# Moving the sign bytes and the taps forward, computing the second double's convolution with three products, and swapping P3 and P7 at the end

## The reference

```python
out = lax.conv_general_dilated(x, weight, window_strides=(1,), padding=[(4, 4)], feature_group_count=4)  # 9 taps
out = out + jnp.einsum('nd,od->no', cond, c_weight)[:, :, None] + bias[None, :, None]
w = kernel.astype(x.dtype) * 2.0 - 1.0            # kernel: (1024, 1024) booleans, so signs +1 and -1
return x + scale * jnp.einsum('bsi,if->bsf', out, w)
```

## Time and profile before

| | us |
|---|---|
| three runs | 174.07, 175.43, 176.49 |
| median | 175.43 |
| the profiled execution | 174.09 |
| its span (first to last instruction) | 172.2 |
| TensorE busy in it | 164.2 |
| VectorE, ScalarE, POOL busy | 136.9, 71.8, 37.6 |

### The profile page before, as it was taken

How to read it: one execution, slowest core, us unless ns; L and a number is a source line. 1 busy time by engine, 2 the same in 40 slices (tenths; PEclk the granted TensorE clock), 3 DMA queues, 4 the chain that set the end, 5 groups by cost and what they waited for, 6 DMA issues and landing times.

```text
span 172.2 us, 2765 instructions
## 1 busy us (share of the span) xinstructions
PE 164.2 (95%) x914; PEld 136.6 (79%) x914; DVE 136.9 (79%) x180; ACT 71.8 (42%) x68; POOL 37.6 (22%) x43
## 2 busy tenths in 40 slices
PE   7699999999999999999999999999999999999791
PEld 2378888998888779887998889887988899888580
DVE  4735493996999999779986899779977997699461
ACT  3201996470791148521781069304842340214000
POOL 4230600005040334006400343043400540000000
PEclk9969999999999999999999999999999999999999
DMA  5688697777799877887977888988888666414006
GB/s 205 139 159 248 249 196 196 125 200 188 143 337 237 256 153 306 184 229 189 297 185 176 262 173 306 225 249 112 331 214 204 94 249 138 105 49 199 0 0 244
DMA packets 27486, 33.38 MB, mean 194 GB/s; under 512 B 3537, under 2 KB 19857, under 8 KB 27473
## 3 DMA queue, kind: packets, MB, share of 16 engines
q1 hardware_dynamic: 22176, 25.63, 54.6%
q10 hardware_dynamic: 4912, 6.78, 14.8%
q0 software_dynamic: 384, 0.81, 2.2%
HBM read 10.06 MB, written 8.40 MB: 107 GB/s over the span
## 4 chain that ended last, share of the span: by engine, by line
PE 92%; DMA 3%; DVE 2%; issue 1%; ACTq 1%; DVEq 0%
PE ps_A L828 30%; PE ps_conv L809 18%; PE ps_C L828 15%; PE ps_conv L786 9%; PE ps_B L828 8%; DMA taps_nat<-weight 3%; PE ps_B L845 2%; PE ps_C L845 2%; PE ps_toep L845 2%; PE ps_A L845 2%; PE ps_toep L828 1%; PE ps_toep L765 1%; PE ps_C L776 1%; PE ps_A L753 1%; DVE sums L250 1%
## 5 line engine op out<-in xcount | busy, mean ns | idle before, releaser
L485 ACT CAST hi<-sums 128x1024 fp32r<-128x1024 f32 x14 | 14.7, 1049 | 44.5 <-DVE sums L622 38.4
L401 POOL TENSOR_TENSOR set<-x_blk 128x512 f32<-128x512 f32 x12 | 17.3, 1461 | 69.7 <-DMA x_blk<-x_phase 69.7
L643 DVE SCALAR_TENSOR_TENSOR x_nat<-ps_A,scale_col,x_nat 128x512 f32<-128x512 f32 x27 | 20.2, 748 | 15.0 <-PE ps_A L828 14.2
L442 ACT COPY x_phase<-x_nat 128x1032 f32<-128x1032 f32 x13 | 27.2, 2135 | 2.2 <-DMA x_nat<-x 2.2
L828 PE MATMUL ps_A<-sign_T,hi 128*128 128x512 f32 x80 | 22.4, 401 | 0.9 <-DVE x_nat L643 0.9
L485 ACT CAST hi<-y_sum 128x1024 fp32r<-128x1024 f32 (+1 forms) x14 | 11.7, 834 | 25.8 <-DMA y_sum<-y_two 16.5
L828 PE MATMUL ps_A<-sign_T,lo 128*128 128x512 f32 x80 | 22.0, 396 | 0.0
L828 PEld LDWEIGHTS ps_A<-sign_T,lo 128*128 128x128 f32 x80 | 15.0, 188 | 3.8 <-DVE lo L632 0.3
L828 PEld LDWEIGHTS ps_A<-sign_T,hi 128*128 128x128 f32 x80 | 14.5, 189 | 4.2 <-issue 1.3
L809 PE MATMUL ps_conv<-toeplitz,w_bytes 128*128 128x128 f32 x144 | 17.2, 276 | 0.4 <-DVE y_two L596 0.4
L809 PEld LDWEIGHTS ps_conv<-toeplitz,set 128*128 128x128 f32 x144 | 16.9, 192 | 0.8 <-issue 0.4
(11 more groups left out here) (108 smaller groups left out, 234.6 us busy)
## 6 DMA issues: line engine op xcount, KB each, us to landing
x_nat<-x SPq DMA_DIRECT2D x16, 512.0 KB, 4.4
out<-x_nat SPq DMA_DIRECT2D x15, 512.0 KB, 4.8
x_blk<-x_phase SPq DMA_DIRECT2D x118, 64.5 KB, 3.0
y_sum<-y_two ACTq DMA_DIRECT2D x48, 128.0 KB, 3.3
w_bytes<-w_bool SPq DMA_DIRECT2D x2, 512.0 KB, 6.5
shift<-shift_dram POOLq DMA_DIRECT2D x2, 256.0 KB, 4.2
x_blk<-x_phase ACTq DMA_DIRECT2D x6, 64.5 KB, 3.7
x_blk<-x_phase POOLq DMA_DIRECT2D x4, 64.5 KB, 3.0
```

The source lines that it names most:

```text
L401: nc.gpsimd.tensor_tensor(dif[r][:, e], x_blk[r][:, :, e:e + M:2], x_blk[r][:, :, e + 1:e + 1 + M:2][:, :, 0:K], ALU.subtract).then_inc(di ...
L442: nc.scalar.copy(x_phase[r][:, :, 0:M + 1], line(d, r, 0, PAD + L + PAD).rearrange("r (m q) -> r q m", q=B)).then_inc(phase_ok[r], B)
L485: nc.scalar.copy(parts(hi_all, k), group(k)).then_inc(hi_ok[k], 1)
L643: nc.vector.scalar_tensor_tensor(there, bank[b], scale2_col[:, :], there, ALU.mult, ALU.add).then_inc(summed[k], 1)
```

## The change

The sign bytes' first half is loaded right behind the first two images; the taps are the first transfer on ScalarE's queue. The blocks of pairs (0, 0) and (0, 1) are spread over the queues in another way, each with its own semaphore, and TensorE takes them in a fixed order. TensorE gets four more warm matmuls ahead of the transposes, the transposes go ahead of the context, and the early shift is made for four rows in place of eight. Signs are made whole, before the first casts. Double 1's convolution is `fast_conv`: everything that makes and takes its operands (`differences`, `odd_blocks`, `fast_y`, `to_parity`) starts at d = 1, and (1, 0)'s blocks are issued by SP and POOL, four each. VectorE's orders in the first double and the last step, and TensorE's P3 and P7 in the last step, are changed. The diff, without what only shifts a counter or an index by one double:

```diff
-WARM = 10, 2
+WARM = 14, 2
-FIRST_BLOCKS = {("SP", 0): (0, 1), ("ACT", 0): (2,), ("POOL", 0): (3,), ("SP", 1): (4,), ("ACT", 1): (5, 6),
-                ("POOL", 1): (7,)}
-EARLY = 8
+FIRST_BLOCKS = {("ACT", 0): (2, 3), ("SP", 0): (0, 1), ("POOL", 1): (4, 5), ("SP", 1): (6,), ("ACT", 1): (7,)}
+FIRST_ORDER = (2, 0, 3, 1), (4, 6, 5, 7)
+EARLY = 4
-CONV_AFTER = {4: 0, 6: 1}
+CONV_AFTER = {5: 0, 7: 1}
...
             load(0, 0, x_first[0])
             load(0, 1, x_first[1])
+            signs_in(sp, 0)
             first_blocks(sp, "SP", 0)
             first_blocks(sp, "SP", 1)
-            signs_in(sp, 0)
             load(1, 0, x_first[2])
             signs_in(sp, 1)
             load(1, 1, x_first[3])
-            to_blocks(1, 0)
+            sp.wait_ge(conv_done[0], 2)
+            sp.wait_ge(phase_ok[0], 2 * B)
+            for a in range(GROUPS):
+                to_block(sp, 0, a, blk_in[0][0])
             load(2, 0, x_in[0])
...
+            pool.wait_ge(conv_done[0], 2)
+            pool.wait_ge(phase_ok[0], 2 * B)
+            for a in range(GROUPS, NG):
+                to_block(pool, 0, a, blk_early)
             pool.wait_ge(shift_out, 16)
...
-            for d in range(2, DOUBLES):
+            for d in range(1, DOUBLES):
                 for r in range(2):
                     differences(d, r)
...
+            act.dma_start(taps_nat[:, :, :], weight).then_inc(taps_in, 16)
             act.dma_start(cond_nat[:, :], cond).then_inc(small_in, 16)
             act.dma_start(cw_nat[:, :], c_weight).then_inc(small_in, 16)
-            act.dma_start(taps_nat[:, :, :], weight).then_inc(taps_in, 16)
...
             def first_double():
 
+                act.wait_ge(w_in[0], 16)
+                sign("B21")
+                sign("B22")
                 high_0("A12")
-                act.wait_ge(w_in[0], 16)
-                sign("B21", KH)
-                sign("B22", 1)
                 high_0("A22")
                 high_0("A11")
                 act.wait_ge(w_in[1], 16)
-                sign("B11", 1)
+                sign("B11")
                 to_phases(1, 1)
-                sign("B12", 1)
+                odd_blocks(1, 0)
+                sign("B12")
                 high_0("A21")
                 to_phases(2, 0)
+                odd_blocks(1, 1)
+                to_parity(1, 0)
+                to_phases(2, 1)
                 high_part("A", 1)
-                to_phases(2, 1)
+                to_parity(1, 1)
+                odd_blocks(2, 0)
                 high_part("S12", 1)
-                odd_blocks(2, 0)
...
                 low_0("A22")
                 low_0("A11")
+                dve.wait_ge(toep_ok, 2)
+                nc.vector.tensor_tensor(toeplitz[:, 2], toeplitz[:, 0], toeplitz[:, 1], ALU.add).then_inc(both_ok, 1)
...
-                sign_sums("T1", plain("B22", LOW), ALU.subtract, plain("T2", LOW), LOW)
-                add_shift(1, 0, 0)
-                sign_sums("T1", plain("B22", HIGH), ALU.subtract, plain("T2", HIGH), HIGH)
-                add_shift(1, 0, 1)
+                sign_sums("T1", plain("B22"), ALU.subtract, plain("T2"))
                 plain_sum("B")
+                fast_y(1, 0)
                 plain_sum("C")
+                plain_sum("E")
+                fast_y(1, 1)
                 low_part("A", 1)
-                add_shift(1, 1, 0)
-                add_shift(1, 1, 1)
                 for k in s_sum:
                     combine(k, 1)
-                plain_sum("E")
                 low_part("S12", 1)
...
                 if last(d):
+                    low_part("S34", d)
+                    for k in ("C22_C", "C12_A", "C12_C", "C22_A"):
+                        sum_up(k, d)
                     finish_last(d)
...
-            def conv(d, r):
...
+            def conv(r):
+                for h in range(2):
+                    if r == 1:
+                        pe.wait_ge(y_ok, 2 * h + 2)
+                    for a in FIRST_ORDER[h]:
+                        g = a - h * GROUPS
+                        pe.wait_ge(blk_first[r][a], 16)
...
+                        if (r, h, a) == (0, 0, FIRST_ORDER[0][0]):
+                            contexts()
+                        if (r, h, a) == (0, 1, FIRST_ORDER[1][0]):
+                            early_shift()
...
                     if n in CONV_AFTER:
-                        conv(1, CONV_AFTER[n])
+                        fast_conv(1, CONV_AFTER[n])
...
                 if last(d):
                     product("P5", d, bank["C"], True, False, "C12_C")
-                product("P6", d, bank["A"], False, False, "C11_P1", 1)
+                    product("P6", d, bank["A"], False, False, "C11_P1", 1)
+                    product("P3", d, bank["C"], False, True, "C22_C", 1)
+                    product("P7", d, bank["A"], False, False, "C12_A", 1)
```

More of the change, by code:

```diff
@@ L221, in wait_blocks @@
             if d == 0:
-                for (of, half), blocks in FIRST_BLOCKS.items():
-                    if half == h:
-                        eng.wait_ge(blk_first[r][of, h], 16 * len(blocks))
+                for a in FIRST_ORDER[h]:
+                    eng.wait_ge(blk_first[r][a], 16)
+            elif (d, r, h) == (1, 0, 1):
+                eng.wait_ge(blk_early, 16 * GROUPS)
             else:
-                eng.wait_ge(blk_in[r][h], 16 * GROUPS * d)
+                eng.wait_ge(blk_in[r][h], 16 * GROUPS * (d - 1 if (r, h) == (0, 1) else d))
         def to_block(eng, r, a, landed):
@@ L237, in first_blocks @@
             for h in range(2):
-                for a in FIRST_BLOCKS[of, h]:
-                    to_block(eng, r, a, blk_first[r][of, h])
+                for a in FIRST_BLOCKS.get((of, h), ()):
+                    to_block(eng, r, a, blk_first[r][a])
         def first_phases(copy, q):
@@ L397, in differences @@
                     wait_blocks(pool, d, r, h)
-                if r == 1:
+                if r == 1 and d > 1:
                     pool.wait_ge(s_ok["S4"], d - 1)
@@ L422, in _, with sign @@
             first_blocks(act, "ACT", 1)
-            def sign(k, pieces):
+            def sign(k):
                 rows = 0 if k[1] == "2" else KH
                 f = int(k[2]) - 1
[L428 to L432, removed]
+                nc.scalar.activation(signs[k][:, :, :], w_bytes[:, rows:rows + KH, f * BANK:(f + 1) * BANK],
+                                     ACT.Copy, bias=-0.5, scale=1.0).then_inc(sign_ok[k], KH)
             def to_phases(d, r):
@@ L456, in to_parity @@
             def to_parity(d, r):
-                act.wait_ge(lo_ok["A" if r == 0 else "A22"], d - 1)
-                for k in (("S2", "S3", "S4") if r == 0 else ("S1", "S3")):
-                    act.wait_ge(s_ok[k], d - 1)
+                if d == 1:
+                    for k in (("A11", "A12") if r == 0 else ("A21", "A22")):
+                        act.wait_ge(lo_0[k], 1)
+                else:
+                    act.wait_ge(lo_ok["A" if r == 0 else "A22"], d - 1)
+                    for k in (("S2", "S3", "S4") if r == 0 else ("S1", "S3")):
+                        act.wait_ge(s_ok[k], d - 1)
                 for p, made in ((0, y_even_ok), (1, y_odd_ok)):
@@ L563, in plain, with add_shift @@
                 return signs[k][:, u, :].bitcast(F32)
-            def add_shift(d, r, i):
-                dve.wait_ge(conv_done[r], 2 * d + i + 1)
+            def add_shift(r, i):
+                dve.wait_ge(conv_done[r], i + 1)
                 if i == 0:
                     dve.wait_ge(early_ok, 1)
-                if d == 1 and i == 0:
-                    for k in (("A11", "A12") if r == 0 else ("A21", "A22")):
-                        dve.wait_ge(lo_0[k], 1)
                 pieces = [(slice(0, B), 2)]
-                if (d, r, i) == (0, 0, 1):
+                if (r, i) == (0, 1):
                     pieces = [(slice(KH, B), 1), (slice(0, KH), 1)]
@@ L611, in combine @@
                 if k in ("S1", "S3"):
[L612 to L615, removed]
-                            dve.wait_ge(y_in[r], 16 * 4 * (d - 1))
+                    for r in range(2):
+                        dve.wait_ge(y_in[r], 16 * 4 * d)
                 if d > 1:
@@ L669, in first_double @@
             def first_double():
[L671 to L673 removed]
+                add_shift(0, 0)
+                add_shift(0, 1)
                 low_0("A12")
[L675 to L676 removed]
+                add_shift(1, 0)
+                add_shift(1, 1)
                 dve.wait_ge(scale_in, 16)
@@ L859, in step @@
                     product("P5", d, bank["C"], True, False, "C12_C")
-                product("P6", d, bank["A"], False, False, "C11_P1", 1)
-                if not last(d):
+                    product("P6", d, bank["A"], False, False, "C11_P1", 1)
+                    product("P3", d, bank["C"], False, True, "C22_C", 1)
+                    product("P7", d, bank["A"], False, False, "C12_A", 1)
+                else:
```

(9 more changed lines are left out.)

85 lines of the change are left out of this document (35 added, 50 removed).

## The result

| | before | changed | ratio, 95% interval |
|---|---|---|---|
| 23 executions each, median us | 175.22 | 177.37 | 1.0074, 1.0049 to 1.0099 |
| lowest, highest us | 173.66, 176.49 | 175.23, 181.57 | |
| changed kernel again, other chip, 6 and 17 | 174.96 | 177.88 | 1.0107, 1.0038 to 1.0177 |

The change makes the kernel slower, by 2.1 us (177.37 against 175.22) in the median, and it spreads: 23 executions of before lie within 2.8 us, those of the changed kernel within 6.3. The profiled execution of the first measurement is the longest of its 23, 181.57 us, and that of the second is the quickest of its six, 175.82 us.

The account below looks back on a forecast made before the run. TensorE, busy for 95% of the span, was taken to bound the kernel. 174.09 + 2.6 (later restart) + 1.3 (clock) - 1.2 (end) = 176.8, and half the 1.34 offset to the median made 177.5 us; range 173.6 to 180.8.

Parts of the forecast that it names:

- The start: First convolutions: earlier taps and more warm matmuls keep the clock at 2.4 GHz; plain products at 17.0, not 19.54, gaining 2.5 us.
- ScalarE's and POOL's queue, VectorE's list: Double 1, r = 0: blocks land at 23.5, fast_y(1, 0) ends at 35.3, though TensorE finished that convolution at 31.
- The transfers: y_two to y_sum in double 1: two rounds in series, landing at 39.9 and 45.1; TensorE waits for A's cast until 41.0.
- VectorE behind S1: S1 to L596 takes 5.2 us, plus 0.5 for POOL's subtractions; fast_conv(2, 1) restarts at 51.5, 2.6 us later than before.
- The clock: TensorE's idle gaps before P2 and fast_conv(2, 1) lower the granted clock: 1.3 us lost, bounds nothing to 1.7.
- The end: Last step: P3 ahead of P7 hides the 0.94 us wait and slower first matmuls: -1.2 us, between -0.9 and -1.4.
- The signs: Listed trace evidence: plain products near 17, S1 near 45, two 3 to 4 us gaps, low clock near 50 to 56.
- A: Rival: queue order is harmless, transfers of r = 1 start at 38.8, restart only 0.4 us later; 173.9 or 174.6; chance 0.17.
- B: Rival: all gains hold (-2.5, -1.8, -1.2), giving 168.6 or 169.3 us; chance 0.05.
- D: Rival: no wait, but the start gains nothing; plain products at 19, restart near 52.8, 178 or 178.8 us; chance 0.06.
- C: Rival: POOL's subtractions delay VectorE's T1 and low part of S12, 1.0 to 1.5 us each; 178.7 or 179.4; chance 0.30.

Follow-up runs that it names:

- e_front_tail: Kernel before with the change's start and end edits, double 1 still convolved by four products: ratio 0.9748 against before, 170.56 us median.
- e_tail: Kernel before with only the last step's new order (P3 ahead of P7, VectorE's sums to match): ratio 0.9865 against before.
- e_parity: Changed kernel with ScalarE issuing the transfers of (1, 1) ahead of A's cast instead of behind it: ratio 0.9955 against before, 174.40 us.

## Why the prediction was right

The time was 177.37 where I said 177.5, and the mechanism is the one foretold: two rounds of transfers in series bring S1 late, the restart of `fast_conv(2, 1)` comes later than before, and the gain at the start is lost there. That the number came so near is partly luck, as errors cancelled. For a profiled execution the sum was 174.09 + 2.6 + 1.3 - 1.2 = 176.8. The profile at 175.82 has 4.0 at the restart, nothing for the clock and -2.3 from there to the end of the span; the one at 181.57 has 7.2, 2.5 and -2.2. How the median's 2.1 us divide between restart and clock stays open, as no profile stands near it. By the steps:

- *The start*: plain products at 17.0, measured 17.2 to 17.6; the clock stays at 2.4 GHz; 2.0 us in timed runs, by `e_front_tail` less `e_tail`.
- *ScalarE's and POOL's queue, VectorE's list*: end of `fast_conv(1, 1)` 37.5 (the terms written there add up to 37.3), measured 37.6; P2 at 41.0, measured 40.7.
- *The transfers*: the first round landed at 39.6 (I said 39.9), the second at 46.8 (45.1). This is the term that was mis-sized: I had taken before's median of 3.3 from issue to landing for both; the second round took 5.2 from the last issue. Between profiles a round takes from 3.4 to 5.6 us, and what sets this isn't settled. For the two issued between 41 and 43 us, where the DMA engines were 0.92 busy, the row below has 4.5. Restart 52.9 instead of 51.5, 4.0 us late and not 2.6.
- *VectorE behind S1*: 5.2 for S1 to L596 was taken, 5.3 measured; S1 and S2 at 0.69. The 0.5 for POOL was not due.
- *The clock*: 1.3 was taken, between 0 and 1.7; it is 0 in one profile and 2.5, outside the bounds, in the other, by whether the restart meets it. That the earlier trace rows show a lower clock at the end, as I wrote, is wrong: only the third slice is below 9.
- *The end*: -1.2 was half of the 2.4 that `e_tail` measured; the order of the last stores has 0.7 of the rest in the profiles.
- *The signs*: the plain products, the clock to 12 us and the end came as listed. S1 is at 46.9, not near 45; the second gap is 1.85, not 3 to 4, since slow products fill it; the clock is low from 41.6 to 48.5, not near 50 to 56. In the execution at 181.57 the gap is 3.81 and the clock low from 56.0 to 61.5.

The landings, DMA view of 41 to 43 us (KB each, median us to landing):

```profile
y_sum<-y_two ACTq DMA_DIRECT2D x2, 128.0 KB, 4.5
```

Rivals: A fell by `e_parity`; B by the gaps; D by the start. C, as the cause of this change's loss, fell by T1 and the low part of S12 in the profile, VectorE then POOL, with the low part of A between them:

```profile
29.77 2.28 DVE L572 TENSOR_TENSOR sign_T<-sign_B,sign_T 128x2048 fp32r<-128x2048 f32 x1
...
40.69 2.00 DVE L638 TENSOR_TENSOR lo<-y_sum,hi 128x1024 fp32r<-128x1024 f32 x1 [2.34 <-ACT hi L493]
...
49.54 1.23 DVE L638 TENSOR_TENSOR lo<-sums,hi 128x1024 fp32r<-128x1024 f32 x1
```

```profile
32.28 2.06 POOL L410 TENSOR_TENSOR w_bytes<-x_blk 128x512 f32<-128x512 f32 x2 [6.90 <-DMA x_blk<-x_phase]
...
49.76 2.92 POOL L410 TENSOR_TENSOR w_bytes<-x_blk 128x512 f32<-128x512 f32 x2 [6.16 <-DVE sums L628]
```

T1 (2.28) and the low part of S12 (1.23) have their full speed. T1 ends before POOL's subtraction starts; at S12 the two overlap, and it is POOL that pays, 2.92 for two subtractions that take 2.06. C's mechanism does act at a third place that I hadn't looked at: the low part of A takes 2.00, and 1.23 in the other execution, beside a subtraction that POOL began at 40.57. It makes the 0.72 before P2's low part, which the second gap covers.

## What to carry to other kernels

A cheaper form of a computation is paid for where its result is first needed: 1.8 us of TensorE were bought with two serial rounds of transfers, at the one place of this kernel where nothing was left to cover them; in the other six doubles the same form makes TensorE wait nowhere but the 0.41 us of the earlier trace rows, with 9 us of products behind it. Before moving one instruction forward, list all the semaphores on which its consumer waits, on every engine, and what now stands behind; freeing one of three made this kernel 2.7% slower. And take the parts of a compound change singly: two of its three parts alone give 2.5%.

## What the hardware showed that I had not expected

- In the execution at 181.57 VectorE's low part of A12 takes 2.58 us, where 0.69 is its time in the other profile; POOL's phase copy runs from 15.50 to 17.56 beside it:

```profile
15.53 2.58 DVE L594 TENSOR_TENSOR lo<-y_sum,hi 128x512 fp32r<-128x512 f32 x1 [0.56 <-ACT hi L479]
...
15.50 2.06 POOL L385 COPY x_phase<-x_nat 128x1032 f32<-128x1032 f32 x1 [4.39 <-DMA x_nat<-x]
```

  The two additions behind it ended 1.1 us later than in the other profile, and T1 started 1.1 later; 0.4 of that is TensorE's later start (plain products at 17.58 for 17.15). In the other profile the low part was first, at 15.48, and the copy, begun at 15.81, took 2.35. So in this pair of executions POOL's copy and VectorE's subtraction hold each other up as POOL's subtractions do.
- Transfers of 128 KB took 3.3 us from issue in the median of both kernels, and 4.5 for the two issued from 41 to 43 us, with the DMA engines 0.92 busy.
- The span doesn't end with the last instruction: 3.1 us pass behind it before, and 2.4 in `e_tail`, where a 512 KB store is out of the way of the last 512 KB. That is 0.7 of the 1.8 us between the two profiles.
